# A four-phase transformer kernel with its loops over sequences and pairs of blocks written out

## What is computed

```python
x = x + attention(layernorm(x))     # 16 heads of 64, latent keys/values of 32, causal softmax
x = x + experts(layernorm(x))       # 8 experts, top 2 by a softmax router, and one shared expert
x = x + scan(layernorm(x))          # Mamba-2 style: conv of 4 taps, 32 heads of 8, chunks of 32
x = x + experts(layernorm(x))       # the same weights again
# experts(x): out[t] = sum over the 2 chosen e of gate * (silu(x Wg_e) * (x Wu_e)) Wd_e
#             + (silu(x Sg) * (x Su)) Sd
```

## Time and profile before

| | |
|---|---|
| median of 3 runs | 3199.05 us |
| the runs | 3197.34 to 3204.44 us |
| the profiled execution | 3181.02 us |
| its span | 3179.0 us |
| TensorE busy | 2622.8 us, 83% |
| VectorE busy | 2036.4 us, 64% |
| ScalarE busy | 1808.9 us, 57% |
| GpSimd busy | 853.9 us, 27% |
| mean TensorE clock granted | 0.888 of full |

### The profile page before, as it was taken

How to read it: one execution, slowest core, us unless ns; L and a number is a source line. 1 busy time by engine, 2 the same in 40 slices (tenths; PEclk the granted TensorE clock), 3 DMA queues, 4 the chain that set the end, 5 groups by cost and what they waited for, 6 DMA issues and landing times.

```text
span 3179.0 us, 76627 instructions
## 1 busy us (share of the span) xinstructions
PE 2622.8 (83%) x26192; PEld 2124.4 (67%) x26193; DVE 2036.4 (64%) x5025; ACT 1808.9 (57%) x4422; POOL 853.9 (27%) x1042
## 2 busy tenths in 40 slices
PE   3999898988989997986886289999999978958882
PEld 2777777777777776775765166667666657857671
DVE  2777666776766765874554666666766647855555
ACT  2777777777777775552444265555665545534441
POOL 0000000000000002663555232342442315744551
PEclk9999999999999997666999599899999876669996
DMA  6323323332332221111222200000000001112225
GB/s 147 48 42 45 48 41 51 49 46 42 49 44 41 41 41 36 40 43 54 69 68 71 88 2 2 2 2 2 2 2 2 2 2 35 41 46 68 70 69 171
DMA packets 117817, 140.22 MB, mean 44 GB/s; under 512 B 21324, under 2 KB 79825, under 8 KB 117360
## 3 DMA queue, kind: packets, MB, share of 16 engines
q1 hardware_dynamic: 100592, 101.63, 17.2%
q0 software_dynamic: 16896, 34.12, 3.2%
HBM read 45.85 MB, written 40.54 MB: 27 GB/s over the span
## 4 chain that ended last, share of the span: by engine, by line
PE 50%; DVE 18%; issue 12%; ACT 9%; another core or an unknown queue 5%; DMA 2%; SPq 1%; DVEq 1%; POOL 1%; ACTq 0%; POOLq 0%
PE psum L457 5%; PE psum L426 5%; PE psum L492 4%; ACT probs L446 3%; PE psum L1515 3%; DVE state L1718 3%; DVE neg_max L435 2%; PE psum L1563 2%; DVE x_sb L1288 2%; PE psum L543 2%; PE psum L1137 2%; PE psum L1432 2%; PE psum L1125 2%; PE psum L304 2%
## 5 line engine op out<-in xcount | busy, mean ns | idle before, releaser
L446 ACT ACTIVATE probs<-psum,neg_max 128x512 f32<-128x512 f32 (+3 forms) x1024 | 539.8, 538 | 244.3 <-DVE neg_max L435 243.5
L435 DVE TENSOR_REDUCE neg_max<-psum 128x1 f32<-128x512 f32 (+3 forms) x1024 | 457.3, 483 | 54.0 <-PE psum L427 24.9
L426 PE MATMUL psum<-ls,qs 96*128 96x512 f32 (+3 forms) x1024 | 380.9, 397 | 112.4 <-ACT probs L446 96.5
L457 PE MATMUL psum<-ident,probs 128*128 128x128 f32 x2560 | 428.4, 283 | 2.9 <-ACT probs L446 0.8
L1250 POOL DMA_INDIRECT y_tok<-yb,xb x272 | 267.7, 984 | 301.5 <-DVE yb L1225 226.6
L426 PEld LDWEIGHTS psum<-ls,qs 96*128 96x128 f32 x1024 | 198.2, 194 | 216.8 <-ACT probs L446 158.4
L325 POOL TENSOR_TENSOR rstd<-var_eps,half_neg 128x4 f32<-128x4 f32 x32 | 40.1, 1254 | 1103.1 <-DVE var_eps L321 1103.1
L476 DVE COPY probs_t<-psum 128x512 f32<-128x512 f32 (+1 forms) x384 | 230.4, 600 | 147.5 <-PE psum L457 140.4
L457 PEld LDWEIGHTS psum<-ident,probs 128*128 128x128 f32 x2560 | 273.7, 144 | 26.1 <-ACT probs_t L472 10.1
L914 POOL DMA_INDIRECT x_slot<-pay,pos_i x256 | 256.3, 1001 | 129.8 <-issue 76.1
L427 PE MATMUL psum<-causal_r,ident_r 128*128 128x128 f32 x1024 | 235.4, 242 | 0.0
(11 more groups left out here) (320 smaller groups left out, 6748.8 us busy)
## 6 DMA issues: line engine op xcount, KB each, us to landing
qs<-q_h SPq DMA_DIRECT2D x128, 256.0 KB, 5.5
xb<-x_slot SPq DMA_DIRECT2D x272, 66.0 KB
qs<-q_l SPq DMA_DIRECT2D x64, 256.0 KB, 5.7
y<-y_tok SPq DMA_DIRECT2D x32, 512.0 KB, 3.5
y_tok<-yb,xb POOLq DMA_INDIRECT x272
x_sb<-in_x SPq DMA_DIRECT2D x16, 256.0 KB, 5.5
x_slot<-pay,pos_i POOLq DMA_INDIRECT x256
out<-x_sb SPq DMA_DIRECT2D x16, 256.0 KB, 2.9
```

The source lines that it names most:

```text
L426: pe.matmul(o[:, at:at + n], q, ls[par][0:3 * LD, 0:n], start=(at == 0), stop=False, skip_group_check=True)
L435: last = dve.tensor_reduce(neg_max[:, par, h, qt:qt + 1], bank[u % 3][:, at:at + (qt + 1) * P], AX.X, ALU.max, negate=True)
L446: last = act.activation(probs[:, u % 3, c], bank[u % 3][:, c], ACT.Exp, bias=neg_max[:, par, h, qt:qt + 1], accum_out=row_sum[:, par, h, q ...
L457: last = pe.transpose(bank[3 + u % 2][:, c:c + P], probs[:, u % 3, c:c + P], ident[:, :])
```

## The change

On PE, DVE, ACT and POOL the hardware loops over sequences and over pairs of blocks become Python loops, so that every turn stands in the program as code of its own. SyncE goes through `with_pairs` too, so its attention loop is written out as well; its loops in the expert phases, VectorE's in the sum and SyncE's at the output stay. What is computed, the buffers and the order of the work don't change. Registers loaded in one turn are now at hand in the next, so that TensorE loads the offsets of experts once for each pair, and no longer for three pairs at the head of a turn.

```diff
@@ -705,7 +705,7 @@
 
             batch(0, 0, 1, True)
             batch(1, 1, 2, True)
-            with eng.Fori(1, PAIRS - 1) as i:
+            for i in range(1, PAIRS - 1):
                 batch(2 * i, 0, 2 * i + 1, True)
                 batch(2 * i + 1, 1, 2 * i + 2, True)
             batch(SEQS - 2, 0, SEQS - 1, True)
@@ -717,7 +717,7 @@
         def route_pairs(eng, batch):
             batch(0, 0, 0, 0, 3)
             batch(1, 1, 1, 0, 3)
-            with eng.Fori(0, (SEQS - 4) // PAY_RING - 1) as i:
+            for i in range(0, (SEQS - 4) // PAY_RING - 1):
                 for k in range(2, 2 + PAY_RING):
                     batch(PAY_RING * i + k, k % 2, k % PAY_RING, i + k // PAY_RING, 3)
             for b in range(SEQS - 6, SEQS):
@@ -1047,7 +1047,7 @@
         def moe_steps(eng, body):
             for st in range(-1, LOOP[0]):
                 body(st, st % RING, st // RING)
-            with eng.Fori(LOOP[0] // RING, LOOP[1] // RING) as i:
+            for i in range(LOOP[0] // RING, LOOP[1] // RING):
                 for j in range(RING):
                     body(RING * i + j, j, i)
             for st in range(LOOP[1], N_PAIR + 2):
@@ -1143,14 +1143,10 @@
             def body(st, j, i):
                 if in_range(st + 1):
                     turn_in(*behind(st, j, i, 1))
-                if not known(st) and j == 0:
-                    for d in (-2, -1, 0):
-                        load_experts(st + d, j + d)
-                if known(st) and st in (0, LOOP[1]):
-                    for p in range(max(st - 2, 0), st + 1):
-                        load_experts(p, p)
+                if st == 0:
+                    load_experts(0, 0)
                 if in_range(st):
-                    hidden(st, j % 2, j, st + 1 < N_PAIR if known(st) else j + 1 < RING)
+                    hidden(st, j % 2, j, st + 1 < N_PAIR)
                 if in_range(st - 1):
                     turn_hidden(st - 1, (j - 1) % 2)
                 if in_range(st - 2):
```

## The result

The changed kernel took 3174.01 us in the median of four runs (3151.6 to 3179.72), the kernel before 3201.74 (3197.34 to 3205.98) beside it: a ratio of 0.9882, 95% interval [0.9842, 0.9921]. The ratio is the comparison's own, worked out over the runs of both kernels, and stands for 38 us; the two medians shown are 27.7 apart. A second set of both kernels (`after_again`) gave 0.9888 [0.984, 0.9936], which is 36 us; its medians, 3169.57 and 3209.11, are 39.5 apart. The forecast was 3170.5 us.

A forecast was written before the change was run, and what follows sets the result against it. TensorE, busy 83% of the span, was taken to wait for code fetches at long loops' jumps. Terms 20.6 + 2 + 2 + 4 = 28.6 us took 3181.0 to 3152.4; the median, 18 us above, was 3170.5, range 3148 to 3190.

The forecast's parts named there:

- Attention, 20.6: Attention loop: five jumps back at 4.13 us each, about 3.0 stall, the rest TensorE at half clock just after.
- the high end, 26.8: Attention: 22.1 us plus 4.7 if two falls of the clock away from any jump go as well.
- its stretches at 70.15 but for one to three of 72.5: Sign expected in attention: one sequence's work takes 70.15 us, in one to three cases 72.5.
- attention's falls of the clock multiply: Sign of being wrong: TensorE's clock falls more often in attention after the change; no size given.
- follow a short idle time that each sequence has: Attention: reason for leaving two falls of the clock, 2.3 to 2.4 us each, out of the 20.6 us.
- Scan, 2: Selective scan: five jumps at 0 to 0.5 us each, 0.4 taken, as TensorE runs ahead of queued work.
- The rival that the jumps cause the scan's long falls (15 us): Selective scan: jumps cause the long half-clock falls, so 15 us more go, to 3155; chance 0.09.
- Routing, 2: Two routing stages, one jump each: sixteen looped sequences at 0.22 us, 3.5 at most, 0 at least, 2 taken.
- Experts, 4: Two expert stages, six jumps each with three offset loads: 12 x 0.3 is 3.6, 4 taken; 0 to 20.4.
- a head costs 0 to 0.6 us: Expert loop: cost of a turn's head, from turns of 30.77 us in the first stage and 30.20 in the second.
- The sequencer has the slack: Expert loop: TensorE is busy only 24.92 of 30.77 us in a turn, so its sequencer has time to spare.
- the rival of 3.5 us a packet: Expert stages: straight code stops TensorE 3.5 us at each of 28 fetched packets, +98 us, to 3268; chance 0.05.

The follow-up runs named there:

- e1_attention: The kernel before with only the attention loop written out, on all five engines; ratio 0.9917, 3164.11 us against 3189.55.
- e9_two_parts: The kernel before with attention and experts written out, scan and routing loops kept; 3157.43 us, ratio 0.9912.
- e6_reload: The changed kernel with the three loads of experts' offsets put back where the turns' heads were, no jump; 3162.91 us, ratio 0.9851.
- e2_scan: The kernel before with only the selective scan's loop written out; ratio 1.0004.
- e7_defer: The changed kernel with VectorE's part of the third to sixth projected block one unit later; 3140.47 us against 3169.57, ratio 0.9788.
- e8_spread: The order of e7_defer with the fourth projected block's scaling another two units later (`32: 3` becomes `34: 3`); 3131.96 us, ratio 0.9833.
- e10_both: The two parts of e9_two_parts with the later scaling of e8_spread; 3139.81 us, ratio 0.9853.

## Why the prediction was right, and where not

**Total.** 3170.5 us forecast, 3174.01 measured, within 3148 to 3190. The sum of 28.6 stands against 27.7 between the medians shown, 39.5 between those of the second set, and 36 to 38 by the ratios. That it meets the first of these to 1 us is in part luck. The new median was to stand 18 us above its profiled execution, as the old one did; it stands 4.6 below (3178.56). And the terms did less well than the sum.

**Attention, 20.6.** The mechanism was right: the jump waits for code. The stalls go with the loop; TensorE's idle time and the packets of the instruction queue go down with the number of jumps. The size is less sure. Within one set or pair of traces attention got shorter by 6.0 (the first pair), 25.0 (`e1_attention`) and 26.6 us (`e9_two_parts`); the part alone won 26.5 by the ratio, with an interval of 16 to 36. The 20.6 lies inside all this, and the high end, 26.8, does too. The Trainium skill's page Advanced Engine Details and Errata, section Control Flow Timing, has about 108 ns for such a branch; of the six in attention only the last (83 ns) is near it, which falls through at the loop's end, while the five that jump back take 3488 to 3896 ns; for a jump in a long body the trace does not agree. The step that failed is the list of what would show it: "its stretches at 70.15 but for one to three of 72.5". In the profile after ten of thirteen are at 71.7 and none at 70.15. One of the prediction's own signs of being wrong, that attention's falls of the clock multiply, came true in this trace. The text had set the falls aside since they "follow a short idle time that each sequence has"; it did not ask how often they could come once no jump shifts them. Executions differ in this: a fall in every sequence of that profile, in about every third of `e1_attention` and `e9_two_parts`, and in the changed kernel's second trace in the first four (71.64 to 71.67 each), then in every third (attention 1046.6 in all). `e6_reload`, with the same code for attention, has none in the first three and one or two in each after them (1053.0 in all).

**Scan, 2.** Measured 0, with an interval of 9 us slower to 6 quicker; inside its bounds of 0 to 2.5 as far as can be told. The rival that the jumps cause the scan's long falls (15 us) is out: `e2_scan` has such sequences without a loop, at 53.1 us.

**Routing, 2.** Writing it out won 1.4 and 2.7 us a stage in the traces of the first and third set, nothing in the second (198.0 looped, 197.9 over six written-out stages), and cost 1.7 and 3.0 in the first pair: from 5 won to 5 lost in all, so the size stays open. The ratio of the part alone would say 8, with an interval of 1 to 15.

**Experts, 4.** This term was mis-sized: 17.5 us by the ratio (10 to 25), 17.9 by the traces of that set (two stages of 254.6 against 244.85 and 246.37), 18.2 and 15.5 in the next two; only the first pair of traces, at 5.2, is near it. The step that failed is "a head costs 0 to 0.6 us", taken from two turns of 30.77 and 30.20 at a clock of 1.00. Both of these turns have a head, so their difference can't price one. At full clock the number was about right all the same: eight straight pairs mostly take 29.9 to 30.5 us, looped ones 30.0 to 30.8. But it could not hold the falls that stand at the heads, because the turns chosen had none; looped turns with falls take up to 32.9 in the middle of a stage. The whole stages have them: a clock of 0.93 to 0.97 looped, 0.97 to 0.99 straight. "The sequencer has the slack" was wrong: TensorE stands idle for 1.4 to 2.1 us at the head, and though other waits shrink by as much, the clock falls. Straight pairs do take their fetches all along the stage, some 17 us apart, a little fewer than the forecast's 2 in 26 us, and the stages got shorter; the rival of 3.5 us a packet is out. The page Runtime: NRT & Kernel Launch of the Trainium skill, section Instruction fetch mechanics, has sequential fetch mostly hidden; by this stage the runs agree.

**What stays open.** The parts' ratios, 0.9917, 0.9945, 0.9975 and 1.0004, sum to 51 us; the whole gives 36 to 38, and `e9_two_parts` 28 where its two parts make 44. The intervals nearly allow it. Falls in step with the sequences would explain 15 to 20 us of it, but only one or two executions of each kernel have a trace, so this is argued and not shown. Nor is it shown what starts the step: `e9_two_parts` ran with granted clocks from 0.888 to 0.897 and times from 3144.66 to 3168.11.

## What to carry to other kernels

Price a loop by the sequencer's view of its jump on each engine and by what is queued behind it: here TensorE's jump took 3.5 us with some 2,800 matmuls and weight loads in the body (two sequences of 705 each), and 0.2 with some 320. A cost that every turn has can't be read from the difference of two turns: compare the loop with straight code. Compare whole stages for clock and busy time and not the quietest turns, because what an idle piece does to the clock after it can be worth more than the piece. And when a stall is removed, look at what period the rest now has: in a program that repeats itself, the falls of the clock can repeat with it.

## What the runs showed of the hardware

The falls of the clock can keep step with a repeating program. In the profile after, ten sequences of 71.7 us had one fall each at the same place. With a longest idle piece of 1.43 us in each sequence, five traces have 5 to 15 falls in attention; with 1.60 us (`e7_defer`) there are 11; with 1.00 us (`e8_spread`, `e10_both`) two each. The sum of the idle time alone doesn't explain it: a sequence at full clock has 5.1 us of it in `e7_defer` and 5.3 in `e8_spread`. Whether it is the length of the longest piece or its place in the sequence isn't shown.

What a removed jump was worth differs more between executions than its stall does. The stall was 2.7 to 3.3 us in each trace. Attention without five of them was shorter by 6.0, 25.0 and 26.6 us, which is 1.2 to 5.3 for each. TensorE's idle time fell by 12 to 13 us in all three; its busy time, which depends on the clock, went up by 7.4 us in the first case, and down by 12.8 and 14.7 in the others.
